# A hybrid transformer layer on one core: the delta path of the new block ahead of the old block's MLP, and twelve scan chunks ahead of attention

## The chip, the core and the metric

The kernel runs on one core of a Trainium2 chip. A core has five engines that run side by side, each through its own list of instructions in order: TensorE (PE, matrix products and transposes), the vector engine (DVE), the scalar engine (ACT), GpSimd (POOL), and SyncE (SP), which here only issues DMA transfers. They meet through semaphores: an instruction can wait until a counter has reached a value, and everything behind it on its engine waits too. The metric is the time of one execution on the device in microseconds; lower is better. The median of three executions stands for the kernel.

## The reference

The input is x of shape (2, 1024, 256), in float32. Four residual steps follow each other:

```
x = x + attn_a(layernorm(x))    # 32 heads of 8, window of 128 keys back
x = x + ffn(layernorm(x))       # 256 -> 1024 -> 256, 4-bit weights plus a low-rank part, relu
x = x + attn_b(layernorm(x))    # delta rule and MLP, below
x = x + ffn(layernorm(x))       # the same weights again
```

The part attn_b normalises (rms), projects to q, k and v, runs a causal convolution of four taps over time, applies silu twice, and scales q and k to unit length per head. Then comes a recurrence over time with one 8 x 8 state per head:

```
err = S @ k_t - v_t
S   = S - beta_t * outer(err, k_t)
o_t = S @ q_t
x   = h + rms(o) @ Wout.T                      # y
x   = x + (silu(g) * u) @ Wdown.T              # g, u = rms(x) @ Wgate.T, @ Wup.T, inner width 704
```

## The kernel before

**Tiling.** Time is cut into NB = 8 blocks of 128 tokens; a block holds both batch rows. Activations stand either as tokens x features or turned as features x tokens. All of the recurrence lives on 128 partitions (2 batch rows x 32 heads x 2 halves of the value rows). Within a block, the scan goes over NC_ = 32 chunks of C = 4 tokens. Each chunk is four operations on DVE in a strict chain (lines 1113, 1120, 1125, 1132 of `scan`); such an operation is called a step here.

**Software pipeline.** Each engine runs `body(t)` for t = -1 to 7. In it the *new* block n = t + 1 passes attention, the first FFN and the delta path (projection, convolution, silu, norms, pair products, til), while the *old* block t passes its scan and then the old block's part: output norm and product, y, MLP, third residual, second FFN, result. Moreover the maxima of the scores of the block after the new one are taken ahead. In body(-1) there is no old block, in body(7) no new one, so seven bodies have both.

**Attention.** 32 units of two heads each. TensorE makes scores (`scores`), ACT the exponentials (`exp_of`), TensorE the values (`values`). Some units also carry a `scores_max` of a later group, of which DVE takes the maximum (`max_unit`). The list PASS1 fixes which. Next to that, DVE works through the scan of the old block. The function `between` places the maxima and the next block's norm between scan steps: MAX_AT, OUT_AT, FRONT_AT and PIECES_AT number the steps as 4 * AHEAD + STEP * unit. So AHEAD is the number of chunks that are done ahead of attention, and STEP the number of scan steps to a unit. Scores need stacks (`k_stack`, `q_stack`) that SP loads by DMA; `next_stacks` waits until enough units of scores are done.

**Behind the convolutions.** This stretch is what the change orders anew. The steps of the delta path of block n:
- ACT `silu_twice(n, s)` for q, k and v, with squares for q and k; TensorE `square_sums(n)`; ACT `l2_norms(n)`, which needs another table than silu (`preload_act_table_set`).
- DVE `units(n)`, then `products(n, 0)` and `products(n, 1)` (products of token pairs in a chunk); TensorE `pairs(n)` brings them to lanes; ACT `pairs_out(n)` copies them; POOL `pair_rows(n)`.
- When the units are done, SP's `to_lanes_dma` writes q, k and v to DRAM and reads them back into lanes. DVE `til_first`, `pair_scale` and `til_column` for j = 0, 1, 2 build what the scan reads; POOL `values_til` copies a part, and DVE `scan` may start.

The steps of the old block t:
- DVE `y_of(t)`; ACT `y_norm(t)`; TensorE `turn_c(t, 1)`; ACT `turn_c(t, 1)`.
- For each of six slices i of the inner width: TensorE `gate_up(t, i)`, ACT `gate_of(t, i)`, DVE `act_of(t, i)`. Two banks alternate, so `gate_up(t, i)` waits for `act_of(t, i - 2)`. Slices 4 and 5 write tiles that `mlp_down(t, 0)` must have read.
- TensorE `mlp_down(t, 0)` and `(t, 1)`; DVE `third_residual(t)`, ACT `norm_c(t)`, DVE `third_apply(t)`; TensorE `turn_c(t, 2)`, then the second FFN (`ffn_c_up`, `ffn_c_down` with ACT `ffn_c`); POOL adds the output bias (`ffn_bias_c`), and DVE `result(t)` ends the block. The second unit of the next attention waits for the result, since it writes the same bank.

Of the kernel before, what the change touches and what calls it, by code (L numbers as in the profile page):

```python
# [27 lines left out]
C = 4  # L28
# [19 lines left out]
STEP = 3  # L48
AHEAD = 3
# [9 lines left out]
def layer_program(nc, a):  # L59
# [9 lines left out]
    with ExitStack() as ctx:  # L69
# [431 lines left out]
        def _(pool):  # L501
# [60 lines left out]
            def body(t, scan=True, following=True):  # L562
# [6 lines left out]
                if scan:  # L569
                    residual(t)  # L570
                    ffn_bias_c(t)
                if following:
                    pair_rows(t + 1)
                    values_til(t + 1)
                pool.sem_clear(gstep)
# [9 lines left out]
        def _(act):  # L585
# [221 lines left out]
            def body(t, scan=True, following=True, front=True):  # L807
# [19 lines left out]
                if scan:  # L827
                    output_squares(t)
                    output_rstd(t)
                    y_norm(t)  # L830
                if scan:
                    turn_c(t, 1)
                if following:
                    silu_twice(n, 0)
                if scan:
                    gate_of(t, 0)
                if following:
                    silu_twice(n, 1)
                if scan:
                    gate_of(t, 1)  # L840
                if following:
                    silu_twice(n, 2)
                if scan:
                    for i in range(2, IT):
                        gate_of(t, i)
# [3 lines left out]
                if scan:  # L849
                    norm_c(t)  # L850
                if following:
                    pairs_out(n)
                if scan:
# [34 lines left out]
        def _(dve):  # L888
# [309 lines left out]
            def body(t, has_scan=True, following=True, front=True):  # L1198
# [56 lines left out]
                if has_scan:  # L1255
                    y_of(t)
                    act_of(t, 0)
                    act_of(t, 1)
                    act_of(t, 2)
                if has_scan:  # L1260
                    act_of(t, 3)
# [3 lines left out]
                if following:  # L1265
                    units(n)
                if following:
                    products(n, 0)
                if has_scan:
                    third_residual(t)  # L1270
                if following:
                    products(n, 1)
                if has_scan:
                    third_apply(t)
                if following:
                    til_first(n)
                    pair_scale(n)
                    for j in range(C - 1):
                        til_column(n, j)
                    scan(n, 0, AHEAD, False, False)  # L1280
# [56 lines left out]
        def _(pe):  # L1337
# [318 lines left out]
            def body(t, scan=True, following=True, front=True):  # L1656
# [16 lines left out]
                if scan:  # L1673
                    turn_c(t, 1)
                    for i in range(IT):
                        gate_up(t, i)
                if following:
                    square_sums(n)
                if scan:
                    mlp_down(t, 0, following)  # L1680
                    mlp_down(t, 1, following)
                if following:
                    pairs(n)
# [112 lines left out]
```

How the kernel before makes its waits and increments, by code:

```python
            def load_x(n):  # L350
                if n >= 2:
                    sp.wait_ge(tm_ready, n - 1)
                sp.dma_start(x_next, x_v[n:n + 1].rearrange("n p b d -> (n p) b d")).then_inc(x_loaded, 16)
# [1 line left out]
            def load_residual(n):  # L356
                sp.wait_ge(x_used, n + 1)
                sp.dma_start(x_in[:], x_v[n:n + 1].rearrange("n p b d -> (n p) b d")).then_inc(x_again, 16)
# [18 lines left out]
            def next_stacks(n, g):  # L378
                sp.wait_ge(scores2, (n * NG + g - RING + 1) * UPG)
                load_stacks(n, g)
                if n == 1 and g < RING:
                    load_pad(1, slot(n, g))
# [1 line left out]
            def pieces_to_dram(n):  # L385
                sp.wait_ge(piece3, n * 2 + 2)
                for p in range(3):
                    sp.dma_start(q_pieces[n:n + 1, p].rearrange("n h p b t -> p (n h) b t"),
                                 pieces[:, 0, p, :].rearrange("p (h b t) -> p h b t", h=HH, b=B)
                                 ).then_inc(pieces_out, 16)
                    for hh in range(HH):
                        sp.dma_start(k_pieces[p, hh, :, :, n * W + W:n * W + 2 * W],
                                     pieces[:, 1, p, hh * BT:(hh + 1) * BT].rearrange("p (b t) -> p b t", b=B)
                                     ).then_inc(pieces_out, 16)
# [1 line left out]
            def load_max(n, g):  # L397
                sp.wait_ge(m_copied, n * NG + g + 1)
                for j in range(3):
# [497 lines left out]
            def done(ins):  # L898
                dve.wait_ge(vstep, mark(ins))
```

## Time and profile before

| | |
|---|---|
| median of three executions | 1532.42 us |
| lowest, highest | 1528.03, 1537.56 us |
| profiled execution | 1531.66 us |
| its span on the core | 1529.9 us |
| TensorE busy | 1123.7 us (73%), mean granted clock 0.836 |
| DVE busy | 927.0 us (61%) |
| ACT busy | 504.9 us (33%) |
| POOL busy | 174.2 us (11%) |

The span is what the trace shows; the execution's time has 1.76 us more around it. A timeline row has the start in us from the span's start, the duration of the merged instructions, the engine, the source line, the operation, output <- inputs by tile name, the shape, and the number of instructions; the square bracket gives the idle time of the engine ahead of it and what ended it.
### The profile page before, as it was taken

How to read it: one execution, taken by the hardware profiler on the slowest of the kernel's cores; microseconds unless marked ns; L12 is line 12 of the kernel's file. 1: busy time of each engine (PE TensorE's matmuls, PEld its weight loads, DVE VectorE, ACT ScalarE, POOL GpSimd, SP SyncE). 2: the span in 40 equal slices, each digit the busy share in tenths (PEclk: the TensorE clock that was granted, in tenths of full speed). 3: DMA queues.
4: the chain of work that ended last, by engine and by line, in shares of the span. 5: the costliest groups of instructions: out<-in, count | busy, mean ns of one | idle time of the engine just before them, and what ended most of it. 6: DMA issues, size and time to landing. Idle time of an engine off the chain costs nothing.

```text
span 1529.9 us, 22243 instructions
## 1 busy us (share of the span) xinstructions
PE 1123.7 (73%) x8586; PEld 744.0 (49%) x8600; DVE 927.0 (61%) x2425; ACT 504.9 (33%) x1043; POOL 174.2 (11%) x251
## 2 busy tenths in 40 slices
PE   5487748687878788787878787878878787676037
PEld 3154515364646555455645554556546554454025
DVE  3613367683758566683768476864768476637831
ACT  1042334234432434224432434334422533242011
POOL 2000000300021000401030000300030003001300
PEclk9588868788979799788988799889988898779559
DMA  9425023401241023401241024201241021001000
GB/s 292 56 39 48 5 68 45 42 22 55 31 54 18 22 69 49 38 22 55 31 54 17 22 69 58 29 22 55 44 48 17 21 64 9 1 14 62 0 14 7
DMA packets 112490, 64.57 MB, mean 42 GB/s; under 512 B 49473, under 2 KB 106753, under 8 KB 112385
## 3 DMA queue, kind: packets, MB, share of 16 engines
q1 hardware_dynamic: 109328, 58.01, 21.9%
q10 hardware_dynamic: 3056, 5.15, 1.1%
q8 instruction: 68, 1.11, 0.3%
q14 instruction: 38, 0.30, 0.1%
HBM read 45.55 MB, written 17.17 MB: 41 GB/s over the span
## 4 chain that ended last, share of the span: by engine, by line
PE 50%; DVE 19%; DMA 11%; SPq 10%; ACT 6%; issue 5%; POOL 1%; DVEq 0%; ACTq 0%; POOLq 0%
PE bank L1624 6%; PE bank L1373 5%; PE bank L1365 5%; PE bank L1475 5%; PE bank L1549 5%; DMA k_stack<-k_pieces 4%; DMA q_stack<-m_rows 4%; DVE conv L1006 4%; PE bank L1647 4%; PE bank L1455 3%; PE bank L1426 3%; PE bank L1345 3%; SPq L369 2%; PE bank L1460 2%; SPq L367 2%
## 5 line engine op out<-in xcount | busy, mean ns | idle before, releaser
L675 ACT ACTIVATE probs<-bank 128x512 f32<-128x512 f32 x256 | 152.0, 597 | 301.9 <-PE bank L1460 301.4
L935 DVE TENSOR_REDUCE mx<-bank 128x2 f32<-128x320 f32 x256 | 121.3, 487 | 152.3 <-PE bank L1426 146.9
L1475 PE MATMUL bank<-probs,v_ext 128*9 128x128 f32 x2048 | 169.5, 288 | 21.4 <-ACT probs L675 16.2
L1421 PE MATMUL bank<-edge_mask,identb 128*128 128x64 bf16 x512 | 62.9, 208 | 121.2 <-DMA k_stack<-k_pieces 82.9
L334 POOL TENSOR_TENSOR lane_buf<-state,q_l 128x128 f32<-128x128 f32 x128 | 86.0, 701 | 401.9 <-DVEq L1138 401.9
L1177 DVE TENSOR_TENSOR hid_c<-bank,probs 128x256 f32<-128x256 f32 (+1 forms) x48 | 19.6, 421 | 163.3 <-ACT probs L792 99.4
L1421 PEld LDWEIGHTS bank<-edge_mask,identb 128*128 128x128 bf16 x512 | 32.7, 100 | 174.5 <-DMA k_stack<-k_pieces 93.4
L1475 PEld LDWEIGHTS bank<-probs,v_ext 128*9 128x9 f32 x2048 | 85.1, 93 | 63.8 <-issue 19.2
L1455 PE MATMUL bank<-tri_mask,identb 128*128 128x512 bf16 x256 | 107.1, 418 | 11.3 <-DMA q_stack<-m_rows 10.6
L1113 DVE TENSOR_TENSOR lane_buf<-state,til 128x128 f32<-128x128 f32 x256 | 102.7, 401 | 18.0 <-POOL lane_buf L559 10.1
L1460 PE MATMUL bank<-q_stack,k_stack 128*128 128x128 bf16 x1024 | 106.7, 231 | 0.0
L1624 PE MATMUL bank<-feat_c,wgu 128*128 128x256 f32 (+1 forms) x384 | 99.4, 423 | 5.4 <-ACT feat_c L635 5.4
L1460 PEld LDWEIGHTS bank<-q_stack,k_stack 128*128 128x128 bf16 x1024 | 84.3, 104 | 36.7 <-issue 10.0
L1426 PE MATMUL bank<-k_stack,q_stack 128*32 128x160 bf16 x2048 | 92.5, 264 | 0.0
L1624 PEld LDWEIGHTS bank<-feat_c,wgu 128*128 128x128 f32 (+1 forms) x384 | 77.7, 207 | 26.6 <-ACT feat_c L635 8.6
L1125 DVE TENSOR_TENSOR state<-u_l,k_l 128x128 f32<-128x128 f32 x256 | 82.2, 321 | 7.5
L1132 DVE TENSOR_REDUCE state<-state 128x32 f32<-128x160 f32 x256 | 81.7, 319 | 6.9
L1120 DVE TENSOR_REDUCE u_l<-lane_buf 128x16 f32<-128x144 f32 x256 | 77.3, 302 | 7.7
L1549 PE MATMUL bank<-feat,w_up 128*128 128x256 f32 x256 | 74.3, 461 | 5.4 <-ACT feat L631 5.4
L1647 PE MATMUL bank<-feat_c,w_up 128*128 128x256 f32 x256 | 61.2, 393 | 10.4 <-ACT feat_c L635 5.4
L1549 PEld LDWEIGHTS bank<-feat,w_up 128*128 128x128 f32 x256 | 58.5, 238 | 21.1 <-ACT feat L631 8.4
L1006 DVE SCALAR_TENSOR_TENSOR conv<-raw,conv_w,conv 128x256 f32<-128x256 f32 x144 | 63.4, 482 | 2.6
(158 smaller groups left out, 1791.0 us busy)
## 6 DMA issues: line engine op xcount, KB each, us to landing
k_stack<-k_pieces SPq DMA_DIRECT2D x192, 64.0 KB
q_stack<-q_pieces SPq DMA_DIRECT2D x192, 32.0 KB
q_l<-lane_q SPq DMA_DIRECT2D x8, 512.0 KB, 4.0
k_l<-lane_k SPq DMA_DIRECT2D x8, 512.0 KB, 4.7
q_pieces<-conv SPq DMA_DIRECT2D x24, 128.0 KB, 2.1
k_pieces<-conv SPq DMA_DIRECT2D x48, 64.0 KB, 2.0
hid<-in_x SPq DMA_DIRECT2D x8, 256.0 KB, 2.8
x_in<-in_x SPq DMA_DIRECT2D x8, 256.0 KB, 2.9
```

The costliest lines, as they stand in the source:

```text
L675: act.activation(probs[:, u % 2], score_bank[u % 2][:], ACT.Exp, scale=float(DK) ** -0.5).then_inc(exp_done, 1)
L935: dve.tensor_reduce(mx[:, g, 2 * v:2 * v + 2], bank[1 + u % 2][:, 0:2 * SPAN].rearrange("p (h k) -> p h k", h=2), AX.X, ALU.max).then_inc( ...
L1006: last = dve.scalar_tensor_tensor(out=dst, in0=src, scalar=w, in1=dst, op0=ALU.mult, op1=ALU.add)
L1113: at = mark(dve.tensor_tensor(first[:, c, :, :, 0:DK], state[:, c, :, :, C].rearrange("p v (o k) -> p v o k", o=1).broadcast_to([128, VR, ...
L1421: pe.matmul(edges[:, :, e * W:e * W + SUB], identb[:], edge_mask[:, e * SUB:(e + 1) * SUB].rearrange("p (o s) -> p o s", o=1) .broadcast_t ...
L1426: last = pe.matmul(pb[s * SUB:(s + 1) * SUB, hp * SPAN:(hp + 1) * SPAN], q_stack[:, r, 2 * v + hp, s * SUB:(s + 1) * SUB], k_stack[:, r, 2 ...
L1455: pe.matmul(pb[:], identb[:], tri_mask[:].rearrange("p (o t) -> p o t", o=1) .broadcast_to([128, 2, 2 * W]), start=True, stop=False, skip_ ...
L1460: last = pe.matmul(pb[:, at:at + W], k_stack[:, r, 2 * v + hp, kb * W:(kb + 1) * W], q_stack[:, r, 2 * v + hp, :], start=False, stop=True, ...
L1475: last = pe.matmul(bank[5][row:row + VE, col:col + W], v_ext[:, b, kb, h, :], probs[:, u % 2, (hp * 2 + kb) * W:(hp * 2 + kb + 1) * W], st ...
L1549: last = pe.matmul(bank[1 + i % 2][:, 0:BT], w_up[:, k, i * 128:(i + 1) * 128], f[:, k], start=(k == 0), stop=(k == KT - 1))
L1624: last = pe.matmul(bank[6 + i % 2][0:m, g * BT:(g + 1) * BT], wgu[:, k, g * INTER + 128 * i:g * INTER + 128 * i + m], fc[:, k], start=(k = ...
L1647: last = pe.matmul(bank[6 + i % 2][:, 0:BT], w_up[:, k, i * 128:(i + 1) * 128], fc[:, k], start=(k == 0), stop=(k == KT - 1))
```

## The change

The functions stay the same; their order in `body` changes on four engines, and the two numbers change.

- ACT: all three `silu_twice` and then `l2_norms` go ahead of `y_norm`; `pairs_out` stands between the second and the third gate.
- DVE: `units` and both `products` follow `y_of`; the til work is interleaved with the act products; the first four scan chunks stand around `third_residual`, in twos, and the next eight ahead of `result`.
- TensorE: `square_sums` goes ahead of `turn_c(t, 1)`, and `pairs` between the second and the third `gate_up`.
- POOL: `ffn_bias_c` goes behind `pair_rows` and `values_til`.
- AHEAD is 12 instead of 3, STEP 2 instead of 3. CUTS[0], the chunk at which the scan pauses after attention, is 28 instead of 27.

```diff
-STEP = 3
-AHEAD = 3
+STEP = 2
+AHEAD = 12
...
@@ POOL body
                     residual(t)
-                    ffn_bias_c(t)
                 if following:
                     pair_rows(t + 1)
                     values_til(t + 1)
+                if scan:
+                    ffn_bias_c(t)
...
@@ ACT body
                     output_rstd(t)
+                if following:
+                    for s in range(3):
+                        silu_twice(n, s)
+                nc.scalar.preload_act_table_set(LOG_EXP_SET)
+                if following:
+                    l2_norms(n)
+                if scan:
                     y_norm(t)
-                if scan:
                     turn_c(t, 1)
-                if following:
-                    silu_twice(n, 0)
-                if scan:
                     gate_of(t, 0)
-                if following:
-                    silu_twice(n, 1)
-                if scan:
                     gate_of(t, 1)
                 if following:
-                    silu_twice(n, 2)
+                    pairs_out(n)
                 if scan:
                     for i in range(2, IT):
                         gate_of(t, i)
-                nc.scalar.preload_act_table_set(LOG_EXP_SET)
-                if following:
-                    l2_norms(n)
-                if scan:
+                    nc.scalar.preload_act_table_set(LOG_EXP_SET)
                     norm_c(t)
-                if following:
-                    pairs_out(n)
...
@@ DVE body
                     y_of(t)
+                if following:
+                    units(n)
+                    products(n, 0)
+                    products(n, 1)
+                if has_scan:
                     act_of(t, 0)
                     act_of(t, 1)
-                    act_of(t, 2)
-                if has_scan:
-                    act_of(t, 3)
+                if following:
+                    til_first(n)
+                    pair_scale(n)
+                for j in range(HALF):
+                    if has_scan and j + 2 < HALF:
+                        act_of(t, 2 + j)
+                    if following and j < C - 1:
+                        til_column(n, j)
                 if has_scan:
                     for i in range(HALF, IT):
                         act_of(t, i)
                 if following:
-                    units(n)
-                if following:
-                    products(n, 0)
+                    scan(n, 0, 2, False, False)
                 if has_scan:
                     third_residual(t)
                 if following:
-                    products(n, 1)
+                    scan(n, 2, 4, False, False)
                 if has_scan:
                     third_apply(t)
                 if following:
-                    til_first(n)
-                    pair_scale(n)
-                    for j in range(C - 1):
-                        til_column(n, j)
-                    scan(n, 0, AHEAD, False, False)
+                    scan(n, 4, AHEAD, False, False)
                 if has_scan:
                     result(t)
...
@@ TensorE body
+                if following:
+                    square_sums(n)
                 if scan:
                     turn_c(t, 1)
-                    for i in range(IT):
+                    gate_up(t, 0)
+                    gate_up(t, 1)
+                if following:
+                    pairs(n)
+                if scan:
+                    for i in range(2, IT):
                         gate_up(t, i)
-                if following:
-                    square_sums(n)
-                if scan:
                     mlp_down(t, 0, following)
                     mlp_down(t, 1, following)
-                if following:
-                    pairs(n)
```

The lists of instructions show where this leaves the rows of an engine. On ACT, the place behind the old block's output norm in every body with both blocks; before (`rs_o` is that norm, `z_c` is y, `sqk` the squares of q and k):

```order
L615 ACTIVATE rs_o<-rs_o 128x256
L780 ACTIVATE probs,lnv_c<-z_c 128x256 x2
L614 ACTIVATE lnt_c<-lnv_c,eps 128x2
L615 ACTIVATE rstd_c<-lnt_c 128x2
L784 ACTIVATE tok_c<-z_c,rstd_c 128x256 x2
L635 COPY feat_c<-bank 128x512
L751 ACT_TABLE_LOAD
L751 ACTIVATE conv<-conv 128x512
```

The same place of the changed kernel:

```order
L616 ACTIVATE rs_o<-rs_o 128x256
L752 ACT_TABLE_LOAD
L752 ACTIVATE conv<-conv 128x512
L753 ACTIVATE conv<-conv 128x512
L756 ACTIVATE sqk<-conv 128x512
L752 ACTIVATE conv<-conv 128x512
L753 ACTIVATE conv<-conv 128x512
L756 ACTIVATE sqk<-conv 128x512
L752 ACTIVATE conv<-conv 128x512
L753 ACTIVATE conv<-conv 128x512
L834 ACT_TABLE_LOAD
L762 ACTIVATE sqk<-bank,eps 128x512
```

Between the output norm and y's norm (before L780, now L781) there are now two table loads, eight activations of silu and squares, and the six of the l2 norms, of which the first is shown.

On TensorE, the difference in the old block's part (`sqk,head_sum` are the square sums, `wgu` the gate products, `to_lanes` the pairs, `wdown_b` the down products):

```order
 L1365 MATMUL bank<-wout_b,q_l 128x256 x4
+L1584 MATMUL bank<-sqk,head_sum 128x512 x2
 L1345 MATMUL bank<-ident,tok_c 128x128 x4
-L1624 MATMUL bank<-feat_c,wgu 128x256 x20
+L1624 MATMUL bank<-feat_c,wgu 128x256 x8
+L1593 MATMUL bank<-hid,to_lanes 128x512 x4
+L1624 MATMUL bank<-feat_c,wgu 128x256 x12
 L1624 MATMUL bank<-feat_c,wgu 64x256 x4
-L1584 MATMUL bank<-sqk,head_sum 128x512 x2
 L1373 MATMUL bank<-wdown_b,hid_c 128x256 x12
-L1593 MATMUL bank<-hid,to_lanes 128x512 x4
 L1345 MATMUL bank<-ident,tok_c 128x128 x4
```

The square sums and the pairs moved up; behind the down products the second turn of the old block follows directly.

On DVE, the place around the third residual of the changed kernel (the four rows L1109 to L1128 are one chunk of the scan, L1180 is the residual, L912 the application):

```order
L1128 TENSOR_REDUCE state<-state 128x32
L1180 TENSOR_TENSOR z_c<-bank,x_c 128x256 x2
L903 BN_STATS stats_c<-z_c 128x6 x2
L906 BN_AGGR mv_c<-stats_c 128x2 x2
L1109 TENSOR_TENSOR lane_buf<-state,til 128x16x8
L1116 TENSOR_REDUCE u_l<-lane_buf 128x16
L1121 TENSOR_TENSOR state<-u_l,k_l 128x32x4
L1128 TENSOR_REDUCE state<-state 128x32
```

A second chunk and then the application follow the last row shown: two chunks now stand between the statistics and the application. Before, the second group of pair products stood there.

## Rows read from the trace of the kernel before

**Rows 1.** Waits of the whole program; who waited for whom: us, times, longest.
```profile
PE bank L1421 <- DMA k_stack<-k_pieces: 82.9, 15, 9.4
...
PE bank L1421 <- DVE mx L935: 17.2, 23, 1.6
```

**Rows 2.** Windows: busy us (instructions) per engine, granted clock, DMA share, GB/s.
```profile
688.00:691.00 3.00, 0.00 (x0) 0.00 (x0) 1.04 (x3) 1.79 (x7) 1.26 (x1) 0.50 0.00 0
```

**Rows 3.** Timeline of TensorE, one period: start, us, instructions, [idle before <- releaser].
```profile
691.68 1.12 PE L1345 MATMUL bank<-ident,tok_c 128*128 128x128 f32 x4 [3.94 <-ACT tok_c L784]
693.47 12.31 PE L1624 MATMUL bank<-feat_c,wgu 128*128 128x256 f32 x48 [0.68 <-ACT feat_c L635]
...
707.53 3.62 PE L1373 MATMUL bank<-wdown_b,hid_c 128*128 128x256 f32 x16
712.05 2.58 PE L1373 MATMUL bank<-wdown_b,hid_c 128*128 128x256 f32 x8 [0.91 <-DVE hid_c L1177]
715.76 1.96 PE L1593 MATMUL bank<-hid,to_lanes 128*128 128x512 f32 x4 [1.12 <-DVE hid L1042]
719.66 2.98 PE L1593 MATMUL bank<-hid,to_lanes 128*128 128x512 f32 x4 [1.95 <-DVE hid L1042]
722.43 1.06 PE L1345 MATMUL bank<-ident,tok_c 128*128 128x128 f32 x4
724.16 5.45 PE L1647 MATMUL bank<-feat_c,w_up 128*128 128x256 f32 x24 [0.68 <-ACT feat_c L635]
...
739.81 0.38 PE L1455 MATMUL bank<-tri_mask,identb 128*128 128x512 bf16 x1
```

**Rows 4.** Timeline of ACT, the same period.
```profile
683.81 0.42 ACT L615 ACTIVATE rs_o<-rs_o 128x256 f32<-128x256 f32 x1
689.08 0.42 ACT L780 ACTIVATE probs<-z_c 128x256 f32<-128x256 f32 x1 [4.84 <-DVE z_c L1169]
...
693.43 1.28 ACT L751 ACT_TABLE_LOAD   x1
694.73 0.63 ACT L751 ACTIVATE conv<-conv 128x512 f32<-128x512 f32 x1
...
707.51 0.69 ACT L761 ACTIVATE sqk<-bank,eps 128x512 f32<-128x512 f32 x1
...
710.97 0.63 ACT L763 ACTIVATE sqk<-sqk 128x512 f32<-128x512 f32 x1
```

**Rows 5.** Timeline of DVE, the same period; last line POOL.
```profile
711.93 1.27 DVE L1026 TENSOR_TENSOR conv<-conv,sqk 128x512 f32<-128x512 f32 x2
...
715.54 0.74 DVE L1184 TENSOR_TENSOR z_c<-bank,x_c 128x256 f32<-128x256 f32 x2
...
717.10 0.25 DVE L910 BATCH_NORM_AGGREGATE mv_c<-stats_c 128x2 f32<-128x6 f32 x2
...
719.53 0.73 DVE L916 TENSOR_SCALAR tok_c<-z_c,mv_c,rstd_c 128x256 f32<-128x256 f32 x2
723.77 1.98 DVE L1052 SCALAR_TENSOR_TENSOR til<-k_l,beta_l 128x1024 f32<-128x1024 f32 x1 [3.51 <-DMA v_l<-lane_v]
...
727.30 1.36 DVE L1076 TENSOR_TENSOR hid<-u_l,til 128x1152 f32<-128x1152 f32 x1
...
733.35 1.11 POOL L559 COPY lane_buf<-til 128x512 f32<-128x512 f32 x1 [7.56 <-DVEq L1081]
```

**Rows 6.** Timeline of TensorE and ACT in the first attention with a scan.
```profile
233.22 1.04 PE L1475 MATMUL bank<-probs,v_ext 128*9 128x128 f32 x8 [14.21 <-ACT probs L675]
...
232.16 0.29 ACT L614 ACTIVATE lnv<-mv,eps 128x2 f32<-128x2 f32 x1 [14.70 <-DVE mv L910]
```

**Rows 7.** Timeline of DVE and TensorE in the last block.
```profile
1409.03 0.76 DVE L1195 TENSOR_TENSOR z_c<-bank,z_c 128x256 f32<-128x256 f32 x2 [1.25 <-PE bank L1373]
...
1452.31 3.35 DVE L1143 TENSOR_REDUCE k_l<-lane_buf 128x256 f32<-128x3072 f32 x1
...
1509.06 7.08 PE L1647 MATMUL bank<-feat_c,w_up 128*128 128x256 f32 x24 [0.68 <-ACT feat_c L635]
```

More of the change, by code:

```diff
@@ L829, in body @@
                     output_rstd(t)
-                    y_norm(t)
-                if scan:
-                    turn_c(t, 1)
                 if following:
-                    silu_twice(n, 0)
-                if scan:
-                    gate_of(t, 0)
-                if following:
-                    silu_twice(n, 1)
-                if scan:
-                    gate_of(t, 1)
-                if following:
-                    silu_twice(n, 2)
-                if scan:
-                    for i in range(2, IT):
-                        gate_of(t, i)
+                    for s in range(3):
+                        silu_twice(n, s)
                 nc.scalar.preload_act_table_set(LOG_EXP_SET)
@@ L849, in body @@
                 if scan:
-                    norm_c(t)
+                    y_norm(t)
+                    turn_c(t, 1)
+                    gate_of(t, 0)
+                    gate_of(t, 1)
                 if following:
                     pairs_out(n)
+                if scan:
+                    for i in range(2, IT):
+                        gate_of(t, i)
+                    nc.scalar.preload_act_table_set(LOG_EXP_SET)
+                    norm_c(t)
                 if scan:
@@ L1672, in body @@
                     output_product(t)
-                if scan:
-                    turn_c(t, 1)
-                    for i in range(IT):
-                        gate_up(t, i)
                 if following:
@@ L1679, in body @@
                 if scan:
+                    turn_c(t, 1)
+                    gate_up(t, 0)
[3 more added lines that the diff above has]
+                if scan:
+                    for i in range(2, IT):
+                        gate_up(t, i)
                     mlp_down(t, 0, following)
                     mlp_down(t, 1, following)
-                if following:
-                    pairs(n)
                 if scan:
```

## The prediction

> **What bounds the kernel now.** I read the waits first. TensorE's largest waits of the whole program are for the stacks that DMA brings for the next block's scores, 82.9 us together, and it waited only 17.2 us for the vector engine's maxima [rows 1]. Attention is therefore paced by TensorE and by stack transfers, which are issued a fixed number of score pairs after attention starts: whatever DVE does ahead of attention cannot shorten it by much. Next comes the timeline of one period (block 4 new, block 3 old; seven periods have both, t = 0 to 6), from the old block's output product to the next attention at 739.81. There the old block's MLP and second FFN are a chain through all engines: DVE adds y, ACT normalises it from 689.08, TensorE turns it at 691.68 and goes on with short gaps to 739.81 [rows 3, 4]. Its longer gaps after 693 are 0.91 (for a product of DVE), 1.12 and 1.95 (for DVE's pair products) [rows 3]. So this stage is set by when y is normalised, then by TensorE's own work; each microsecond that y comes later is a microsecond of the period, unless work leaves TensorE's chain in exchange.
>
> **The change: y's norm now stands behind the delta path on ACT.** All times are on the clock of that period, up to ACT's last step ahead of the edit, which ends at 683.81 + 0.42 = 684.2 [rows 4].
> - ACT used to idle 4.84 us, start the y norm at 689.08 and let TensorE turn at 691.68, 2.6 later [rows 3, 4]. Now it first loads the silu table (1.28), runs eight silus and squares of 0.63 with some 0.03 between them (5.3), loads the other table (1.28) and does the six steps of the two l2 norms (707.51 to 711.60, 4.1) [rows 4]. 684.2 + 1.3 + 5.3 + 1.3 + 4.1 = 696.2. Its inputs don't delay it: the third silu begins at 689.5, and the third convolution is over before DVE's y, which ends at 689. The square sums follow the output product on TensorE; both took at most 1.8 between 705.8 and 707.5 [rows 3], say 3.5 at the low clock, the second behind its square at 689.5, so they end before 693, and ACT asks at 692.1 for the first, done by 691, and at 694.2 for the second. The y norm starts at 696.2, not 689.1: **7.1 us later**; the turn is at 698.8. The edit fills a hole of 4.8 us with 12 us of work.
> - From the turn to the end of the six gate products TensorE took 691.68 to 693.47 + 12.31 = 705.8, 14.1, with the low clock at its start [rows 3]: at 688 to 691, in its idle time, the granted clock is 0.50, the 1.2 GHz level [rows 2]. The engine is again idle before the turn, so I take the same 14.1, plus the pair matmuls now between the second and third gate product, two groups of 1.96 at the high clock [rows 3], 3.9. Their inputs on DVE, units and products, took 711.93 to 715.54 and then 717.35 to 719.53, 5.8 in all [rows 5]; even begun at 696.2 they are ready at 702, before TensorE asks. 698.8 + 14.1 + 3.9 = 716.8.
> - A wait is added: DVE's fourth act product stands behind the first til column (two operations of 1.36 [rows 5]), and the sixth gate product needs that bank. The lanes arrived 10.6 us after the units (713.2 to 723.77 [rows 5]), so now, units ending near 696.9, at 707.5. The til step, the scaling and the state copy take 727.30 - 723.77 = 3.5, to 711.0. A gate product, at the 0.227 of the FFN's matmuls [rows 3], takes 1.8, so the third ends at 711.4 and its act product at 712.3; the column ends at 715.1, the fourth act product at 715.6. TensorE asks at 715.0: 0.6. The gates end at 717.4.
> - The MLP's down products with two act products between them took 707.53 to 714.63 = 7.1 [rows 3]: 724.5. The square sums, which stood before them, are off this chain.
> - **The third residual has lost its cover.** It ran on DVE from 715.54 to its application's end at 720.3, while TensorE did the pairs until 722.4 [rows 3, 5]. Now TensorE has nothing else. Residual and statistics took to 717.35, 1.8; then two scan chunks stand before the application. A chunk is (1452.31 - 1409.79) / 29 = 1.47 [rows 7], two are 2.9; the application is 0.73 [rows 5]. 724.5 + 1.8 + 2.9 + 0.7 = 729.9: the second turn comes at 729.9 and not at 722.43, **7.5 late**. TensorE idles 5.4 us there.
> - From that turn to attention it took 739.81 - 722.43 = 17.4 [rows 3]. The first 24 of the FFN's matmuls ran in 5.45 us; in the last block, behind a longer idle time, in 7.08 [rows 3, 7]. I add that 1.6. Attention starts **9.1 us late in each of seven periods: +63.7**.
> - DVE's eight further chunks (4 to 11) take 11.8 and end near 742, under the second FFN, some 7 us before its result is asked for; without that cover they would hold the result and attention's second unit. SP's lane loads and next input go 14 us earlier, and behind them stands only the output store. POOL now does the rows and the til copy (1.11 [rows 5]) ahead of the bias, which has 15 us until the result. I cost these at nothing.
>
> **First and last block.** In the first attention TensorE stands 14.21 us behind an exp, which is behind ACT's wait of 14.70 for DVE's next-block variance, itself behind the til work and the chunks [rows 6]. Nine chunks more are 13.2, and STEP puts the variance one scan step of 0.37 earlier: **+12.9**. At the end DVE alone goes from 1409.79 to 1452.31 over 29 chunks, now 20: 9 x 1.47 = **-13.2** [rows 7]. In the attention blocks the closer spacing of the maxima can give back no more than part of the 17.2 of waits, bounds 0 and -17; most of these lie outside the scan's stretch, so I take -1.
>
> **Sum.** 63.7 + 12.9 - 13.2 - 1 = +62.4 on a span of 1529.9. The profiled execution took 1531.66, 1.76 more than its span and 0.76 under the median: 1532.4 + 62.4 = **1595**.
>
> **A page against the rows.** The added table loads are 1.28 us each in the trace and the next activation starts 0.02 after the load (693.43 + 1.28, 694.73) [rows 4]. The Trainium skill (ScalarE: Activation LUTs, "What ACT_TABLE_LOAD costs") has a load of about 1283 ns and a drain of some 1380 ns with it, about 2.66 us a switch. By it, two loads ahead of y would cost 2.8 us more a period and the sum would be some 19 higher, an estimate from that page; the rows show no such pause.
>
> **The rivals.**
> 1. *As above* (0.80). Own range 1565 to 1618: at the low end the clock costs nothing (-11), the fourth act product doesn't wait (-4) and the chain gains 2 us a period elsewhere (-14); at the high end it is 3.3 us a period later than taken, as it would be with the lanes or the chunks slower than their rows.
> 2. *No change within 1%* (0.09), about 1532 to 1547. The 7.5 are 7.1 for y and 0.6 for the act product, less 1.7 of square sums, plus 5.4 + 3.9 for idle time and pairs in place of the 7.8 between 714.6 and 722.4. If the residual found a cover, its 5.4 and the clock's 1.6 would go, 2.1 a period would stay (+15), and with y late by only 5 none. For it: the waits of 1.12 and 1.95 do vanish. Against it: nothing stands on TensorE between the down products and the turn.
> 3. *Faster* (0.06), about 1505. DVE, not TensorE, sets the pace of attention, with three scan steps (1.1 us) and often a maximum to a unit; nine chunks fewer are 13.2 us, less the 9.1: -4.1 x 7 = -29 beside first, last and median. It decides once more than 9.1 us of an attention is DVE's. Against it: 17.2 us in the whole program [rows 1].
> 4. *A pause behind each table load* (0.05). The two activations behind the loads ahead of y start 1.4 us late each: 2.8 x 7 = 19, 1614. Against it: 694.73 in the rows. (It is the page's rule above.)
>
> Slower by over 1%: 0.85 (1 and 4); within 1%: 0.09; faster: 0.06. 1% is about what a measurement of this kernel can tell from no change. The range is that of case 1 and holds case 4.
>
> **What would show it.** In the changed profile ACT's y squares start some 7 us after DVE has added y, with no idle time before them; TensorE waits some 7 us for that turn, and some 5 for the turn behind the third application; DVE idles some 7 us ahead of the result; the waits for stacks stay near 83; the first attention's wait grows from 14 to 27; the last scan takes some 29 us. I am wrong if attention gets shorter by more than a microsecond, if ACT reaches the y norm before 693 on this clock, or if the second turn follows the down products without a wait.

## The result, and the profile after

| | before | changed |
|---|---|---|
| median of 4 executions each, same comparison | 1531.34 us | 1591.97 us |
| lowest, highest | 1528.03, 1537.56 | 1589.18, 1601.91 |
| ratio | | 1.040, 95% interval 1.0352 to 1.0448 |
| span of the profiled execution | 1529.9 us | 1600.1 us |
| mean granted clock in it | 0.836 | 0.831 |

The changed kernel is 4.0% slower, some 61 us (54 to 69 by the interval); 1595 was forecast. The profiled execution is the longest of the changed kernel's; the others had spans of 1587.4 to 1590.9. So the two traces differ by 70.2 us and the timings by 61. What part of that surplus the traces explain is said below the table; where two kernels are compared in size, the ratios decide.

What TensorE waited for in the whole program of the changed kernel (total us, times, longest):

```profile
PE bank L1421 <- DMA k_stack<-k_pieces: 84.3, 15, 10.0
...
PE bank L1345 <- ACT tok_c L785: 55.3, 8, 7.8
PE bank L1345 <- DVE tok_c L912: 41.9, 8, 5.5
PE bank L1475 <- ACT probs L676: 28.1, 8, 25.8
...
PE bank L1421 <- DVE mx L931: 17.7, 26, 1.6
...
PE bank L1440 <- DVE mpieces L947: 11.2, 8, 1.5
```

The stacks are where they were, 84.3 against 82.9 [rows 1], and so are the maxima, 17.7 against 17.2. The first turn of the old block (L1345 behind ACT) waits 55.3 us in eight blocks, up to 7.8 a time; before, it was 30.6 us, 3.94 of them in the block of [rows 3]. The second turn (L1345 behind DVE) waits 41.9; before, it waited once, 3.3 us in the last block. The line of `mpieces` is new.

The timeline of TensorE in the same period as before (t = 2, so old block 2 and new block 3; the prediction, counting from one, calls them 3 and 4), from the first turn to the next attention:

```profile
728.01 1.11 PE L1345 MATMUL bank<-ident,tok_c 128*128 128x128 f32 x4 [7.70 <-ACT tok_c L785]
729.80 5.29 PE L1624 MATMUL bank<-feat_c,wgu 128*128 128x256 f32 x16 [0.68 <-ACT feat_c L636]
734.93 3.60 PE L1593 MATMUL bank<-hid,to_lanes 128*128 128x512 f32 x8
738.36 5.34 PE L1624 MATMUL bank<-feat_c,wgu 128*128 128x256 f32 x24
744.37 1.94 PE L1624 MATMUL bank<-feat_c,wgu 128*64 128x256 f32 x8 [0.67 <-DVE hid_c L1173]
...
750.87 2.58 PE L1373 MATMUL bank<-wdown_b,hid_c 128*128 128x256 f32 x8 [0.91 <-DVE hid_c L1173]
758.97 1.12 PE L1345 MATMUL bank<-ident,tok_c 128*128 128x128 f32 x4 [5.52 <-DVE tok_c L912]
760.76 6.90 PE L1647 MATMUL bank<-feat_c,w_up 128*128 128x256 f32 x24 [0.68 <-ACT feat_c L636]
...
777.86 0.38 PE L1455 MATMUL bank<-tri_mask,identb 128*128 128x512 bf16 x1
```

These rows answer to [rows 3]: the first turn waits 7.70 us, the pairs stand among the gates and have no wait, the sixth gate waits 0.67 for the fourth act product, and the second turn waits 5.52. ACT in the same period, from the last step of the output norm to y's first square, answers to [rows 4]:

```profile
713.40 0.42 ACT L616 ACTIVATE rs_o<-rs_o 128x256 f32<-128x256 f32 x1
713.83 1.28 ACT L752 ACT_TABLE_LOAD   x1
715.13 0.63 ACT L752 ACTIVATE conv<-conv 128x512 f32<-128x512 f32 x1
...
720.12 1.28 ACT L834 ACT_TABLE_LOAD   x1
721.41 0.69 ACT L762 ACTIVATE sqk<-bank,eps 128x512 f32<-128x512 f32 x1
...
725.41 0.40 ACT L781 ACTIVATE probs<-z_c 128x256 f32<-128x256 f32 x1
```

There is no idle time in brackets: ACT works without a gap from 713.83 to y's squares at 725.41, 11.6 us. DVE around the third residual and at the result answers to [rows 5]:

```profile
753.60 0.76 DVE L1180 TENSOR_TENSOR z_c<-bank,x_c 128x256 f32<-128x256 f32 x2
...
755.18 0.25 DVE L906 BATCH_NORM_AGGREGATE mv_c<-stats_c 128x2 f32<-128x6 f32 x2
...
758.18 0.74 DVE L912 TENSOR_SCALAR tok_c<-z_c,mv_c,rstd_c 128x256 f32<-128x256 f32 x2
...
778.11 0.76 DVE L1191 TENSOR_TENSOR z_c<-bank,z_c 128x256 f32<-128x256 f32 x2 [7.80 <-PE bank L1373]
```

The residual starts with the end of the down products; two chunks stand between 755.18 and 758.18; at the end DVE has done its twelve chunks and idles 7.80 us before the result. The granted clock behind the two waits (the number behind the POOL column; then DMA share and GB/s):

```profile
728.00:731.00 3.00, 2.32 (x7) 1.74 (x8) 2.96 (x9) 1.82 (x2) 0.00 (x0) 0.50 0.66 190
758.97:761.00 2.03, 1.35 (x5) 0.95 (x6) 1.86 (x6) 0.59 (x1) 1.48 (x2) 0.50 0.00 0
```

Both turns start at 0.50, the 1.2 GHz level. Lastly the first attention (TensorE and ACT) and the last block (DVE: result of block 6, and first half of the outputs of block 7), which answer to [rows 6, 7]:

```profile
243.70 1.04 PE L1475 MATMUL bank<-probs,v_ext 128*9 128x128 f32 x8 [25.80 <-ACT probs L676]
...
242.63 0.29 ACT L615 ACTIVATE lnv<-mv,eps 128x2 f32<-128x2 f32 x1 [26.29 <-DVE mv L906]
...
1491.57 0.76 DVE L1191 TENSOR_TENSOR z_c<-bank,z_c 128x256 f32<-128x256 f32 x2 [7.72 <-PE bank L1373]
...
1521.92 3.35 DVE L1139 TENSOR_REDUCE k_l<-lane_buf 128x256 f32<-128x3072 f32 x1
```

The wait in the first attention is 25.80 instead of 14.21. The last block's scan takes 1492.33 to 1521.92, 29.6 us, for its 20 chunks.

**Where the 70.2 us between the two traces are.** From the timelines I took for each old block the start of y's addition on DVE, of both turns and of the next attention on TensorE, and averaged over the blocks. The last column gives the sum over the blocks.

| stretch | before | changed | difference x blocks |
|---|---|---|---|
| y to first turn | 3.32 | 9.84 | 6.52 x 7 = 45.6 |
| first turn to second | 30.75 | 31.40 | 0.65 x 7 = 4.6 |
| second turn to attention | 17.37 | 19.47 | 2.10 x 6 = 12.6 |
| attention to next y, five full | 118.55 | 119.50 | 0.95 x 5 = 4.8 |
| the same, the last attention | 108.95 | 110.85 | 1.9 |
| span's start to the first y | 347.0 | 358.6 | 11.6 |
| second turn of block 6 to y of block 7 | 87.3 | 76.0 | -11.3 |
| y of block 7 to the end | 51.2 | 51.6 | 0.4 |

They sum to 70.2. Two thirds is the delay of y alone.

Not all of the 70.2 belongs to the change. Up to the first y, the traces of silu_first, y_delay, products_first and products_warm (below) run the same instructions as the kernel before, and their first y comes at 351.2 to 352.6 us, not at 347.0; apply_first runs those of the changed kernel, and there it comes at 365.8, not at 358.6. So that row is uncertain by several microseconds. In all nine traces of this document the average of the five full attentions lies between 118.1 and 119.5 us, and the last attention takes 104.5 to 110.9.

### The profile page after: what moved, and what is told of

Its sections match the earlier page's. It is cut to its first block, busy times and chain, and to the rows that moved or that the text cites. A ratio compares the mean times of both kernels' runs of the same rounds, so it can differ in the third digit from the quotient of the medians.

```text
span 1600.1 us, 22279 instructions
## 1 busy us (share of the span) xinstructions
PE 1138.6 (71%) x8586; PEld 756.4 (47%) x8600; DVE 936.8 (59%) x2425; ACT 525.8 (33%) x1058; POOL 174.3 (11%) x251
## 3 DMA queue, kind: packets, MB, share of 16 engines
q8 instruction: 68, 1.11, 0.3%
## 4 chain that ended last, share of the span: by engine, by line
PE 50%; DVE 17%; DMA 12%; ACT 10%; SPq 8%; issue 3%; POOL 1%; DVEq 0%; ACTq 0%; POOLq 0%
PE bank L1475 6%; PE bank L1373 6%; PE bank L1365 5%; PE bank L1647 5%; PE bank L1549 5%; DMA k_stack<-k_pieces 5%; DMA q_stack<-m_rows 4%; PE bank L1624 4%; PE bank L1455 3%; PE bank L1426 3%; PE bank L1574 3%; PE bank L1460 3%; PE bank L1345 2%; PE bank L1421 2%; DVE lane_buf L1109 2%
## 5 line engine op out<-in xcount | busy, mean ns | idle before, releaser
L1421 PE MATMUL bank<-edge_mask,identb 128*128 128x64 bf16 x512 | 62.9, 208 | 119.2 <-DMA k_stack<-k_pieces 84.3
L1475 PEld LDWEIGHTS bank<-probs,v_ext 128*9 128x9 f32 x2048 | 85.2, 92 | 74.1 <-ACT probs L676 30.3
L1624 PE MATMUL bank<-feat_c,wgu 128*128 128x256 f32 (+1 forms) x384 | 103.5, 430 | 11.3 <-DVE hid_c L1173 5.9
L1109 DVE TENSOR_TENSOR lane_buf<-state,til 128x128 f32<-128x128 f32 x256 | 100.2, 391 | 6.7 <-POOL lane_buf L559 1.3
L1128 DVE TENSOR_REDUCE state<-state 128x32 f32<-128x160 f32 x256 | 81.9, 320 | 8.1
L1345 PE MATMUL bank<-ident,tok_c 128*128 128x128 f32 x64 | 17.5, 427 | 97.2 <-ACT tok_c L785 55.3
L1647 PE MATMUL bank<-feat_c,w_up 128*128 128x256 f32 x256 | 75.1, 458 | 10.4 <-ACT feat_c L636 5.4
L1121 DVE TENSOR_TENSOR state<-u_l,k_l 128x128 f32<-128x128 f32 x256 | 77.4, 302 | 6.8
L1647 PEld LDWEIGHTS bank<-feat_c,w_up 128*128 128x128 f32 x256 | 57.6, 235 | 27.9 <-ACT feat_c L636 8.6
```

The source lines that it names most:

```text
L1109: at = mark(dve.tensor_tensor(first[:, c, :, :, 0:DK], state[:, c, :, :, C].rearrange("p v (o k) -> p v o k", o=1).broadcast_to([128, VR, ...
L1421: pe.matmul(edges[:, :, e * W:e * W + SUB], identb[:], edge_mask[:, e * SUB:(e + 1) * SUB].rearrange("p (o s) -> p o s", o=1) .broadcast_t ...
L1475: last = pe.matmul(bank[5][row:row + VE, col:col + W], v_ext[:, b, kb, h, :], probs[:, u % 2, (hp * 2 + kb) * W:(hp * 2 + kb + 1) * W], st ...
L1624: last = pe.matmul(bank[6 + i % 2][0:m, g * BT:(g + 1) * BT], wgu[:, k, g * INTER + 128 * i:g * INTER + 128 * i + m], fc[:, k], start=(k = ...
L1647: last = pe.matmul(bank[6 + i % 2][:, 0:BT], w_up[:, k, i * 128:(i + 1) * 128], fc[:, k], start=(k == 0), stop=(k == KT - 1))
```

## The experiments

The theory: the order behind the convolutions costs its nine microseconds a period, most of it because ACT normalises y late, some because the third residual lost its cover, some through TensorE's clock; the twelve chunks ahead only move time from the last block to the first attention. The rivals: the chunks and the spacing cost it; y's delay is absorbed; DVE paces attention. Ratios are against the kernel before in the same comparison: silu_first, apply_first, ahead3 and products_first shared one with it at 1536.45 us (median of 9), y_delay, after_warm and products_warm one at 1534.85 (median of 9). One per cent is 15 us.

### silu_first: the silus of ACT's part alone

```diff
                 if scan:
                     output_squares(t)
                     output_rstd(t)
+                if following:
+                    for s in range(3):
+                        silu_twice(n, s)
+                    if scan:
+                        nc.scalar.preload_act_table_set(LOG_EXP_SET)
+                if scan:
                     y_norm(t)
-                if scan:
                     turn_c(t, 1)
...
```

> The kernel before with one part of the change alone: ACT does the three silus of the new block, with a table load on either side, ahead of the old block's y norm; l2 norms, DVE, TensorE and POOL stay as before. Theory: ACT is through at 684.2 + 1.3 + 5.3 + 1.3 = 692.1 on the clock of the period shown, 3.0 us after y; every microsecond of that passes into the period: 3.0 x 7 = +21, 1552 us. Rival (y's delay is hidden by later waits, as the pair waits of 3.1 us would allow): 1531 to 1535. Rival (a pause of 1.4 us behind each load): 1572.

Measured: 1552.50 us, ratio 1.0097 (1.0062 to 1.0131), +15 us. ACT from the first table load to y's squares, and TensorE's first turn:

```profile
692.61 1.28 ACT L751 ACT_TABLE_LOAD   x1
...
698.90 1.28 ACT L834 ACT_TABLE_LOAD   x1
700.19 0.42 ACT L780 ACTIVATE probs<-z_c 128x256 f32<-128x256 f32 x1
...
702.79 1.12 PE L1341 MATMUL bank<-ident,tok_c 128*128 128x128 f32 x4 [6.77 <-ACT tok_c L784]
```

From the load at 692.61 to the squares at 700.19 ACT takes 7.6 us, and the turn waits 6.77. Over seven blocks, y to first turn is 5.84 instead of 3.32, 2.5 later each, 17.6 us in all; the timing shows 15, its interval 10 to 20, against 21 expected. The delay passes into the time; whether all of it does, the interval leaves open. The rival by which the pair waits absorb it is out: those waits are 30.4 us in this trace, 30.3 before. So is the pause behind table loads: the squares start 0.01 behind the load (698.90 + 1.28).

One thing here nobody had expected. In four of the seven blocks the FFN's first products took 7.35 to 7.54 us instead of 5.45, though the second turn starts without a wait. In the same period:

```profile
735.30 7.35 PE L1643 MATMUL bank<-feat_c,w_up 128*128 128x256 f32 x24 [0.68 <-ACT feat_c L635]
```

The granted clock from 735.3 to 739 is 0.50. So TensorE can be at the low clock in the FFN without a long wait at the second turn.

### y_delay: y late as in the change, nothing moved

```diff
                     output_rstd(t)
+                    if following:
+                        for _ in range(27):
+                            done(act.copy(sq[:], w_up[:, 0, 0:D]))
                     y_norm(t)
```

> The kernel before with nothing moved, but with 27 copies of 128x256 on ACT between the old block's output norm and y's norm, whose result nobody reads (some 0.42 us each with the gap, 11.3 us, of which 4.8 fall into ACT's idle time): y's norm comes some 6.5 us later, as in the changed kernel, and all else stays. Theory: every microsecond passes into the seven periods, 6.5 x 7 = +46 on the kernel before, 1577 to 1582 us, and some 8 more if the longer idle time costs clock in the FFN too; that would be three quarters of the whole loss, the uncovered residual the rest. Rival (the pair waits of 3.1 us and DVE's waits absorb a part of it): +20 to +25.

Measured: 1583.12 us, ratio 1.0346 (1.0302 to 1.0389), +53 us (46 to 60). ACT's copies, then TensorE's two turns and the gates of one block:

```profile
699.88 11.73 ACT L832 COPY probs<-w_up 128x256 f32<-128x256 f32 x27
...
714.25 1.11 PE L1348 MATMUL bank<-ident,tok_c 128*128 128x128 f32 x4 [10.73 <-ACT tok_c L784]
716.04 12.30 PE L1627 MATMUL bank<-feat_c,wgu 128*128 128x256 f32 x48 [0.68 <-ACT feat_c L635]
...
745.00 1.06 PE L1348 MATMUL bank<-ident,tok_c 128*128 128x128 f32 x4
```

The copies took 11.73 us, and y to first turn is 9.78 on average against 3.32: 6.46 later, times 7 = 45.2. On average the rest of the block is as before: first turn to second 31.06 (before 30.75), second turn to attention 17.10 (17.37). Block by block it is not: in four of the seven the gates took 13.0 us and the first group of pairs 3.75 instead of 1.96, and TensorE's waits for pair products fell to 22.3 us in the whole program, from 30.3. What those waits took up went to slower matmuls, and from y to the second turn every block is 6.4 to 6.9 us longer. The rival (+20 to +25) is out. With nothing else changed, the kernel has lost most of what the change lost. So the delay of y on ACT makes up some 45 of the 61 us. The timing shows 8 us more than that, and its interval begins just above the 45. The span of the trace is 50.0 us longer than before, 4.6 of them ahead of the first y, where both kernels are the same.

### apply_first: the third residual without the two chunks in it

```diff
                 if has_scan:
                     third_residual(t)
-                if following:
-                    scan(n, 2, 4, False, False)
                 if has_scan:
                     third_apply(t)
                 if following:
-                    scan(n, 4, AHEAD, False, False)
+                    scan(n, 2, AHEAD, False, False)
```

> The changed kernel with the two chunks between the third residual and its application moved behind the application. Theory: TensorE's second turn comes 2.9 us earlier, less the 0.6 that ACT's two steps then take in the open: -2.3 x 7 = -16, 1576 us; down to 1565 if the shorter idle time also keeps the clock up. Rival (the residual isn't on the path, the y norm alone is): 1592.

Measured: 1579.99 us, ratio 1.0257 (1.0194 to 1.032), against 1.040 for the changed kernel: some 22 us less, 16 expected, and the intervals of the two don't meet. The size is loose: two of its four executions lie at 1573 us, the other two at 1587 and 1588. DVE's application, and TensorE's second turn and first FFN products:

```profile
758.80 0.74 DVE L912 TENSOR_SCALAR tok_c<-z_c,mv_c,rstd_c 128x256 f32<-128x256 f32 x2 [0.60 <-ACT rstd_c L616]
...
759.60 1.00 PE L1343 MATMUL bank<-ident,tok_c 128*128 128x128 f32 x4 [3.36 <-DVE tok_c L912]
761.27 8.06 PE L1645 MATMUL bank<-feat_c,w_up 128*128 128x256 f32 x24 [0.68 <-ACT feat_c L636]
```

The application now waits 0.60 for ACT, and the second turn 3.36 instead of 5.52. First turn to second is 29.20 against 31.40: 2.2 x 7 = 15. The residual was on the path; two chunks in its middle cost what they take, less the 0.6 that ACT needs anyway. But the FFN's first products are slow here as well, 8.06 us, and second turn to attention is 19.40, as in the changed kernel (19.47): with the wait cut from 5.52 to 3.4 the loss in the FFN stayed.

The 53 us of y_delay and the 22 of this run are more than the 61 of the whole change. The change also removes something, the waits for the pairs of 1.12 and 1.95 a period [rows 3]; what that gives back by itself, no run isolates.

### ahead3: the chunks back to three

```diff
-STEP = 2
-AHEAD = 12
+STEP = 3
+AHEAD = 3
...
                 if following:
-                    scan(n, 2, 4, False, False)
+                    scan(n, 2, AHEAD, False, False)
                 if has_scan:
                     third_apply(t)
-                if following:
-                    scan(n, 4, AHEAD, False, False)
```

> The changed kernel with AHEAD = 3 and STEP = 3 again; its order behind the convolutions stays, with chunks 0 and 1 ahead of the third residual and chunk 2 behind it. My theory (the order costs some 9 us a period, the chunks ahead of attention only move time from the last block to the first attention): the first attention gets 12.9 us back, the last block loses 13.2, and one chunk less ahead of the application gives 1.44 x 7 = 10: 1592 - 10 = 1582 us. Rival A (the twelve chunks and the closer spacing cost the time, the order is neutral): back to 1531. Rival B (DVE paces attention, and the twelve chunks had hidden part of the order's cost): over 1620.

Measured: 1595.78 us, ratio 1.0364 (1.0318 to 1.0409), by the ratios 5 us under the changed kernel (by the medians 4 above it), with intervals that meet; 10 were expected, which the timing can't tell from 5. Both rivals are out: the time goes neither back to 1531 nor beyond 1620. The trace has the two displaced pieces. The first attention's wait (the longest of the three numbers; total, times, longest) is back:

```profile
PE bank L1473 <- ACT probs L676: 17.3, 8, 15.1
```

And y of block 6 to y of block 7 took 129.5 us, against 117.1 in the changed kernel: 12.4 us come back at the end, 10.7 (25.80 less 15.1) leave at the start. First turn to second is 29.88, 1.5 a period less, for the one chunk that no longer stands ahead of the application. Attention to next y is 118.65 with nine chunks more in it than in the changed kernel (119.50) and in apply_first (118.61); before, also with three chunks ahead, it was 118.55. It doesn't matter to attention how many chunks DVE has left for it.

### after_warm: does the clock take part?

```diff
+            def filler(n, sem_, count, times):
+                pe.wait_ge(sem_, count)
+                for _ in range(times):
+                    pe.matmul(bank[3][:], identb[:], tri_mask[:].rearrange("p (o t) -> p o t", o=1)
+                              .broadcast_to([128, 2, 2 * W]), start=True, stop=True, skip_group_check=True)
...
+                if scan and following:
+                    filler(n, raw_ready, n * 3 + 3, 18)
                 if scan:
                     turn_c(t, 1)
...
+                if scan and following:
+                    filler(n, pairs_copied, n + 1, 20)
                 if scan:
                     turn_c(t, 2)
```

> The changed kernel with matmuls whose result nobody reads, 18 of 512 columns ahead of the first turn of the old block and 20 ahead of the second, so that TensorE isn't idle in its two long waits (7.7 and 5.5 us). Theory of the clock: gates and FFN then run at the high clock from their start; the gates have 1.8 us to gain (12.31 against six times 1.75), the turn 0.5, the FFN 2.1: up to -4.9 x 7 = -34 on the changed kernel, 1558 us; with half of it 1575. Rival (the clock plays no part in the loss, or the filling delays the turns): 1592 or more.

Measured: 1585.61 us, ratio 1.0352 (1.0302 to 1.0402): 7 us under the changed kernel, with intervals that meet, and nowhere near 1558. The fillers are the rows L1660:

```profile
715.32 4.05 PE L1660 MATMUL bank<-tri_mask,identb 128*128 128x512 bf16 x18
723.16 1.11 PE L1345 MATMUL bank<-ident,tok_c 128*128 128x128 f32 x4 [3.79 <-ACT tok_c L785]
...
748.85 6.08 PE L1660 MATMUL bank<-tri_mask,identb 128*128 128x512 bf16 x20
754.77 0.60 PE L1345 MATMUL bank<-ident,tok_c 128*128 128x128 f32 x4
756.04 5.45 PE L1647 MATMUL bank<-feat_c,w_up 128*128 128x256 f32 x24 [0.68 <-ACT feat_c L636]
```

I had sized them badly. The first 18 took 4.05 us and left 3.79 of idle time, behind which the turn again takes 1.11, the time of the low clock. The second 20 took 6.08 in the block shown, more than the wait, and so the turn starts about half a microsecond late; but then it takes 0.60 and the FFN's first products 5.45 instead of 6.90. That is one block. In the other six the fillers took 4.49, and the turn followed after 1.10 of idle time in 0.66; even so the FFN's first products took 7.13 in five of them and 5.45 in one. Old block 3:

```profile
932.84 7.13 PE L1647 MATMUL bank<-feat_c,w_up 128*128 128x256 f32 x24 [0.68 <-ACT feat_c L636]
```

The granted clock was 1.00 in the fillers (925.91 to 930.40) and 0.53 from 932.84 to 936. The second turn to attention came down from 19.47 to 18.09 on average, with 16.9 to 17.0 in two of the six blocks and 18.66 in the others. So the two microseconds that the FFN lost in the changed kernel are the clock's: they come back where it stays up. But filling the wait up to its last 1.1 us didn't keep it up in five of seven blocks, and the run doesn't settle what both waits could give back with other fillers.

### products_first: one small piece of the idea, on the kernel before

```diff
                     products(n, 0)
+                    products(n, 1)
                 if has_scan:
                     third_residual(t)
-                if following:
-                    products(n, 1)
```

> The kernel before, with the second group of pair products ahead of the third residual on DVE. Theory: the second group of pairs follows the first on TensorE without the wait of 1.95 us, the residual's application comes 2.2 + 1.8 + 0.6 + 0.7 us after the first group, near 720.7 on the clock of the period shown, when TensorE is through with the pairs at 720; the second turn comes some 1.8 us earlier and the clock stays high: -1.8 to -2.8 x 7, 1511 to 1519 us. Rival (the application, now later, is what TensorE waits for, and nothing is gained): 1531.

Measured: 1523.01 us, ratio 0.99 (0.9865 to 0.9935), 15 us faster than the kernel before; 12 to 20 were expected. TensorE's two groups of pairs, the second turn and the FFN's first products:

```profile
719.39 1.96 PE L1594 MATMUL bank<-hid,to_lanes 128*128 128x512 f32 x4 [1.13 <-DVE hid L1042]
721.61 1.98 PE L1594 MATMUL bank<-hid,to_lanes 128*128 128x512 f32 x4 [0.26 <-DVE hid L1042]
724.67 0.66 PE L1346 MATMUL bank<-ident,tok_c 128*128 128x128 f32 x4 [1.08 <-DVE tok_c L916]
726.01 5.45 PE L1648 MATMUL bank<-feat_c,w_up 128*128 128x256 f32 x24 [0.68 <-ACT feat_c L635]
```

The second group waits 0.26 instead of 1.95 [rows 3]; in exchange the turn waits 1.08 for the application. So it is in six of the seven blocks; in old block 0 the pairs ran at the low clock and nothing was gained between the turns (31.01). On average the turn is 1.1 us earlier, and the turn itself takes 0.66 and not 1.06, since the clock doesn't fall between the groups. First turn to second is 29.67 (30.75), second turn to attention 16.97 (17.37).

### products_warm: the same, with fillers ahead of the first turn

The diff is products_first with the filler of after_warm, ten matmuls ahead of the first turn only.

> The kernel before with the second pair products ahead of the residual, and 10 unread matmuls of 512 columns on TensorE ahead of the first turn of the old block, in a wait of 3.9 us. Theory: clock high from the gates' start, -1.8 to -2.3 us a period on top of the 13 that the products gave: 1523 - 14 = 1509 us. Rival (at the low clock the ten take 4.3 us, longer than the wait, and delay the turn by what they gain): 1523.

Measured: 1514.01 us, ratio 0.9883 (0.9845 to 0.9921), 18 us faster than the kernel before; 9 us under products_first by the medians, but by the ratios, whose intervals overlap, only 3. The expected 14 are not shown, and whether the fillers gain anything in the time isn't settled. Fillers (L1661), turn and first gates, and then the second attention unit:

```profile
685.03 3.62 PE L1661 MATMUL bank<-tri_mask,identb 128*128 128x512 bf16 x10
688.60 0.66 PE L1346 MATMUL bank<-ident,tok_c 128*128 128x128 f32 x4
689.94 3.72 PE L1625 MATMUL bank<-feat_c,wgu 128*128 128x256 f32 x16 [0.68 <-ACT feat_c L635]
...
736.90 0.62 PE L1476 MATMUL bank<-probs,v_ext 128*9 128x128 f32 x8 [1.98 <-DVE z_c L1195]
```

The turn follows the fillers without a wait here (in two of seven blocks; in the others it waits 0.4 to 1.2), takes 0.66, and the first two gates take 3.72 in all seven, instead of the 5.29 in the changed kernel's row. First turn to second is 28.30, 1.4 less than in products_first. In exchange a wait for DVE begins to show: attention's second unit waits 1.98 for the result, which stands behind the third scan chunk; in the whole program that is 5.0 us, 0.6 before.

## Why the prediction was right, point by point

- **Attention isn't paced by DVE.** Right. Nine chunks fewer in it changed nothing (apply_first, 118.61, against 118.65 in ahead3 and 118.55 before), and the waits for stacks stayed.
- **y 7.1 us late.** The mechanism is shown (y_delay, silu_first), the size was 6.5 on average, 6.7 in five of the seven blocks. The step that was too large is ACT's string: 12.0 us were forecast, 11.6 measured; activations of different instructions follow each other a little closer (715.13 to 720.12 is 5.0 for the eight, not 5.3).
- **Pairs among the gates: no wait, 3.9 us.** Right, 3.60 in the row. **Fourth act product: 0.6.** 0.67.
- **Residual without cover, 5.4.** 5.52, and apply_first shows that its chunks are on the path. **Second turn 7.5 late:** 6.52 + 0.65 = 7.2.
- **FFN 1.6 slower through the clock.** 2.1 on average, and the clock's part is shown (after_warm). The forecast laid it to the idle time at the second turn, and that is not shown: the products were as slow in four blocks of silu_first and one of y_delay without a wait there, and in five of after_warm behind 1.10 us. What brings the clock down stays open. **Attention 9.1 late a period:** 9.3.
- **First attention +12.9.** The wait grew by 11.6. The chunks came as priced (1.44 each), but in this execution the lanes arrived earlier: DVE's first til step waited 5.60 us for them instead of 6.63.
- **Last block -13.2.** The scan is 42.52 - 29.59 = 12.9 shorter. The -11.3 of the table starts at the second turn of block 6, and so has the slower FFN of that block in it (6.83 us against 5.45).
- **Attention blocks -1.** Wrong in sign, if small, and a mechanism was missed. With STEP = 2 the four pieces of the maxima, one to a scan step, spread over two units instead of one and a third, and TensorE's turn of them at unit 22 waits for the last: 11.2 us in all, up to 1.54 each. The wait stands in the three traces with STEP = 2 and not in ahead3. It costs little, because the stack wait behind it takes it up. TensorE in the changed kernel's next attention:

```profile
815.62 0.24 PE L1440 MATMUL bank<-identb,mpieces 128*48 128x128 bf16 x1 [1.54 <-DVE mpieces L947]
...
824.79 0.29 PE L1421 MATMUL bank<-edge_mask,identb 128*128 128x64 bf16 x2 [7.29 <-DMA k_stack<-k_pieces]
```

1.54 and 7.29 are 8.8 together; before, the stack wait alone was 8.96 in that block. In apply_first, with the same AHEAD and STEP, attention to next y is 118.61, as before, so the 0.95 that the changed kernel's trace has more is not the spacing. It lies mostly with the stacks: in the five full attentions TensorE's waits for DMA add up to 59.5 us in the changed kernel's trace and to 55.1 in that of apply_first, 4.4 of the 4.5 us between them. Why the stacks came later in that execution isn't shown.

The total is nearer than its terms deserve: 1595 lies 3 us from the median, while the interval of the timing is 7 us to either side, and one term had the wrong sign. What carries the forecast is the 63.7 for the periods, against which the table's first three rows have 62.8.

The rivals: "no change" needed a cover for the residual; there was none. "Faster" needed DVE as attention's pace (its own terms sum to 1502 or 1503, not to the 1505 given; nothing hangs on that). The pause behind table loads is absent: 713.83 + 1.28, next activation at 715.13; 720.12 + 1.28, next at 721.41; nor is there one ahead of the load (713.40 + 0.42, load at 713.83). The drain of some 1380 ns a switch in the Trainium skill (ScalarE: Activation LUTs, "What ACT_TABLE_LOAD costs") would have added 19 us, an estimate from that page; these rows don't have it, and the measurement decides.

## What to carry to other kernels

An engine's idle hole can take only the work that fits in it: ACT had 4.8 us before y's norm and got 11.6 us, and the rest went straight into the path, since the chain behind it had no slack. Before moving work ahead, look at what the moved work had covered as well (here the pairs hid the third residual), and at which engine waits in the stretch that is to get shorter; attention had no use for chunks done ahead. The part of the idea that was worth having was small and local: the second group of products ahead of the residual, 1% faster. The clock is a term of its own: it took two microseconds from the same matmuls in some blocks of a run and not in others, so look at every block before reading one row as the rule.

## What the runs showed of the hardware

- The granted clock decides about two microseconds of a stretch of 17: the same 24 FFN matmuls take 5.45 us in seven blocks of the kernel before (at 1.00 in the period shown) and 6.83 to 8.43 in seven of the changed one, where the clock is 0.54 in the first 3.2 us of the period shown (760.76 to 764). Cutting the wait ahead of the turn from 5.5 to 3.4 us gave none of it back (6.86 to 8.25 in apply_first).
- A long wait just ahead is not needed for the low clock: it was 0.50 in the FFN of silu_first (735.3 to 739) with no wait at the turn, and 0.53 in after_warm (932.84 to 936) although TensorE had run fillers at 1.00 until 930.40 and idled 1.1 us. The same stretch of the same execution stayed up in some blocks and fell in others.
- At its first wait TensorE is at the low clock already (0.50 from 688 to 691 [rows 2]; 0.50 from 704 to 714 in y_delay). A longer wait there cost little more: the gates took 12.30 in y_delay behind a wait of 10.73 us and 13.0 in four blocks behind 9.65, against 12.31 before behind 3.94.
- A table load on ACT cost its 1.28 us and nothing behind it where ACT had no other wait: the next activation starts 1.30 and 1.29 us after the load in the changed kernel, 1.29 in silu_first.
